# A new order of the steps in the start-up of a Mamba-2 and feed-forward kernel

## The reference

```python
x = x + _layernorm(mamba2(_layernorm(x)))        # in_proj, causal conv of 4 taps, SSM scan, gate, norm, out_proj
x = x + _layernorm(ffn(_layernorm(x)))           # 256 -> 2048 -> 256
```

## Time and profile before

| | us |
|---|---|
| three runs | 996.67, 999.93, 1002.15 |
| median | 999.93 |
| the profiled execution | 997.25 |
| its span | 995.5 |
| PE, DVE, ACT, POOL busy | 893.7, 776.1, 603.5, 341.3 |

### The profile page before, as it was taken

The page is one execution under the profiler, slowest core; times in us unless marked ns, Lnnn a source line. Parts: engine busy times, 40 slices in busy tenths (PEclk is TensorE's granted clock), DMA queues, the critical chain, the costliest instruction groups (busy, mean ns, idle before and its releaser), DMA issues.

```text
span 995.5 us, 17481 instructions
## 1 busy us (share of the span) xinstructions
PE 893.7 (90%) x6304; PEld 771.7 (78%) x6304; DVE 776.1 (78%) x2031; ACT 603.5 (61%) x1017; POOL 341.3 (34%) x342
## 2 busy tenths in 40 slices
...
DMA packets 19205, 34.57 MB, mean 35 GB/s; under 512 B 2480, under 2 KB 11440, under 8 KB 19120
## 3 DMA queue, kind: packets, MB, share of 16 engines
...
q10 hardware_dynamic: 864, 0.03, 0.1%
...
## 4 chain that ended last, share of the span: by engine, by line
PE 54%; DVE 22%; ACT 8%; issue 7%; POOL 5%; DMA 3%; SPq 0%; DVEq 0%; POOLq 0%; ACTq 0%
PE fb L1082 24%; PE db L1082 12%; PE mb L1082 10%; DVE xc L890 4%; DVE lmat L864 2%; PE mb L1191 2%; DMA lmat<-rows 2%; PE mb L1182 2%; DVE hid L999 2%; PE mb L1197 1%; POOL hl L588 1%; PE mb L1172 1%; POOL yg L576 1%; ACT hl L717 1%; DMA wg_raw<-in_packed 1%
## 5 line engine op out<-in xcount | busy, mean ns | idle before, releaser
L588 POOL TENSOR_TENSOR hl<-hid,hl 128x512 fp32r<-128x512 f32 (+1 forms) x144 | 171.2, 1189 | 415.3 <-ACT hl L717 415.3
L1082 PE MATMUL fb<-x1t,wg 128*128 128x512 f32 (+1 forms) x864 | 218.4, 389 | 5.2 <-DVE x1t L993 5.2
L1082 PE MATMUL db<-wd,hl 128*128 128x256 f32 x1536 | 213.7, 289 | 2.0 <-POOL hl L588 2.0
L1082 PE MATMUL fb<-x1t,wu 128*128 128x512 f32 (+1 forms) x864 | 205.0, 374 | 7.2 <-ACT hid L710 7.1
L1082 PEld LDWEIGHTS db<-wd,hl 128*128 128x128 f32 x1536 | 197.4, 191 | 16.7 <-issue 9.1
L1082 PEld LDWEIGHTS fb<-x1t,wu 128*128 128x128 f32 x864 | 151.6, 192 | 42.4 <-ACT hid L710 14.6
L1082 PEld LDWEIGHTS fb<-x1t,wg 128*128 128x128 f32 x864 | 148.1, 195 | 35.5 <-issue 8.7
L999 DVE TENSOR_TENSOR hid<-fb,hid 128x512 f32<-128x512 f32 (+1 forms) x144 | 90.4, 628 | 90.0 <-PE fb L1082 76.8
L717 ACT ACTIVATE hl<-hid 128x512 fp32r<-128x512 f32 (+1 forms) x144 | 83.6, 581 | 98.2 <-DVE hid L999 69.6
L890 DVE SCALAR_TENSOR_TENSOR xc<-raw,cw,xc 128x256 f32<-128x256 f32 x288 | 133.6, 532 | 8.2 <-ACT xc L663 7.0
L710 ACT ACTIVATE hid<-fb 128x512 f32<-128x512 f32 (+1 forms) x144 | 78.1, 548 | 78.2 <-PE fb L1082 75.0
(11 more groups left out here) (140 smaller groups left out, 1347.0 us busy)
## 6 DMA issues: line engine op xcount, KB each, us to landing
...
```

Source lines behind the costliest of these rows:

```text
L588: pool.tensor_tensor(hl[:, hs, n % 2, 1, :], hid[:, hs, n % 2, :], hl[:, hs, n % 2, 0, :].bitcast(F32), ALU.subtract).then_inc(s["lo"], 1)
L1082: last = pe.matmul(ps, lhs(a, k), rhs(b, k), start=start and n == 0, stop=stop and n == len(todo) - 1, skip_group_check=check)
```

## The change

The text of `FIRST` is written anew for PE, ACT, DVE and POOL. Each list holds the same steps as before, each of them once: 108 on PE, 145 on ACT, 154 on DVE, 46 on POOL. `ORDER`, `LAST` and all functions stay. The table is one line longer, so that every line behind it has a number one higher. One line of the diff, the first of ACT's list, as a sample:

```diff
@@ -102,47 +102,48 @@
 FIRST = {
...
     "act": """
-        wi_split:0 rates:0 dq:0 wi_z:0 xn_split:1 taps:3 dq:1 dq:2 gate:3 dq:3 dl:0 taps:4 dq:4 gate:4 dq:5 dq:6
...
+        wi_split:0 xn_split:1 wi_z:0 rates:0 taps:3 wo_split:0 dq:0 silu:3 taps:4 dq:1 gate:3 dt_bias:1 dq:2
...
```

More of the change, by code:

```diff
@@ L104 @@
     "pe": """
[L105 to L109, removed]
@@ L110 @@
-        yt:3> gu:14 dn:12 out:3> gu:15 x1t:0> dn:13 z:0>> z:1>> ip:0>> x1t:1> dn:14 ip:1>> dn:15 ip:2>> z:2>>""",
-    "act": """
-        wi_split:0 rates:0 dq:0 wi_z:0 xn_split:1 taps:3 dq:1 dq:2 gate:3 dq:3 dl:0 taps:4 dq:4 gate:4 dq:5 dq:6
[L113 to L125, removed]
@@ L126 @@
-    "dve": """
[L127 to L139, removed]
@@ new lines @@
+        xt:1 ip:3 ip:4 z:3 z:4 z:5 ip:5 cs:1 ct:1 xtr:2 gb:1 yo:2 st:2 yd:2 xt:0> xtr:3 yt:2 yo:3 out:2 yd:3
+        yt:3 st:3 out:3 z:0> z:1> ip:0> ip:1> ip:2> x1t:1 cs:0> z:2> gu:0 ct:0> gu:1 gu:2 xtr:0> yo:0> gb:0>
+        gu:3 yd:0> dn:0 st:0> dn:1 yt:0> xtr:1> gu:4 out:0> yo:1> dn:2 gu:5 yd:1> st:1> gu:6 xt:1> dn:3 yt:1>
+        dn:4 ip:3> gu:7 out:1> z:3> z:4> dn:5 gu:8 ip:4> ip:5> cs:1> dn:6 gu:9 z:5> ct:1> xtr:2> gb:1> gu:10
+        dn:7 xt:0>> dn:8 gu:11 yo:2> dn:9 st:2> yd:2> gu:12 xtr:3> yt:2> dn:10 gu:13 yo:3> out:2> dn:11 yd:3>
@@ new lines @@
+        gu:14 dn:12 yt:3> gu:15 st:3> out:3> z:0>> z:1>> x1t:0> dn:13 dn:14 ip:0>> ip:1>> z:2>> x1t:1> dn:15
+        ip:2>>""",
+    "act": """
+        wi_split:0 xn_split:1 wi_z:0 rates:0 taps:3 wo_split:0 dq:0 silu:3 taps:4 dq:1 gate:3 dt_bias:1 dq:2
+        gate:4 gate:5 dl:0 dq:3 dq:4 silu:4 dq:5 taps:5 dl:1 dq:6 dl:2 silu:5 dq:7 dq:8 dl:3 exps:1 decay_sums:4
+        decay_sums:5 decay_matrix:4 decay_matrix:5 gb_copy:1 decay_sums:6 decay_matrix:6 decay_sums:7
+        xn_split:0> square:2 yt_split:2 decay_matrix:7 square:3 yt_split:3 dq:9 dl:4 dt_bias:0> gate:0> taps:0>
+        gate:1> taps:1> x1_split:1 taps:2> gelu:0 gelu:1 split:0 dl:5 dl:6 gelu:2 gate:2> silu:0> silu:1>
+        silu:2> decay_sums:0> exps:0> decay_matrix:0> decay_sums:1> split:1 decay_matrix:1> decay_sums:2>
+        decay_matrix:2> gb_copy:0> decay_sums:3> decay_matrix:3> gelu:3 split:2 yt_split:0> square:0> dl:7 dq:10
+        split:3 dl:8 gelu:4 dl:9 gelu:5 split:4 gelu:6 xn_split:1> yt_split:1> split:5 taps:3> square:1> gelu:7
+        split:6 dl:10 dt_bias:1> split:7 gate:3> gate:4> gelu:8 taps:4> dq:11 taps:5> silu:3> gate:5> silu:4>
+        silu:5> gelu:9 split:8 decay_sums:4> gb_copy:1> decay_sums:5> gelu:10 decay_sums:6> exps:1> split:9
+        decay_matrix:4> decay_matrix:5> decay_sums:7> xn_split:0>> decay_matrix:6> split:10 decay_matrix:7>
+        gelu:11 square:2> split:11 gelu:12 yt_split:2> dl:11 gelu:13 split:12 gelu:14 yt_split:3> square:3>
+        split:13 gelu:15 split:14 dt_bias:0>> gate:0>> split:15 x1_split:0> gate:1>> taps:0>> x1_split:1>
+        taps:1>> taps:2>>""",
@@ new lines @@
+    "dve": """
+        stats1:1 xn:1 xn_split:1 wi_split:0 rates:0 wo_split:0 wo_lo:0 conv:3 dq:0 dt_bias:1 conv:4 stats1:0>
+        scale:0 dq:1 dq:2 scale:1 softplus:1 dq:3 scale:2 dq:4 decays:1 conv:5 dl:1 dl:2 xn:0> dq:5 dq:6 dq:7
+        scale:3 xdt:2 dl:3 scale:4 sums:1 dl:0 gb_copy:1 scale:5 yoff:2 decayed_products:2 dq:8 state:2 ydiag:2
+        xn_split:0> xdt:3 yt_split:2 decayed_products:3 yoff:3 stats2:2 ydiag:3 ln2:2 yt_split:3 state:3 dq:9
+        scale:6 stats2:3 x1n:2 dt_bias:0> ln2:3 softplus:0> x1n:3 conv:0> decays:0> x1_split:1 conv:1> inter:0
+        scale:7 inter:1 conv:2> sums:0> dl:5 dl:4 scale:8 xdt:0> gb_copy:0> yoff:0> inter:2 decayed_products:0>
+        stats1:1> scale:9 ydiag:0> state:0> decayed_products:1> yt_split:0> inter:3 xdt:1> xn:1> stats2:0> dq:10
+        yoff:1> inter:4 ln2:0> ydiag:1> state:1> xn_split:1> inter:5 scale:10 yt_split:1> inter:6 dl:6 x1n:0>
+        dl:7 stats2:1> inter:7 dt_bias:1> ln2:1> softplus:1> conv:3> decays:1> conv:4> conv:5> stats1:0>>
+        sums:1> inter:8 dq:11 gb_copy:1> inter:9 scale:11 xn:0>> dl:10 dl:8 dl:9 xdt:2> inter:10
+        decayed_products:2> yoff:2> xn_split:0>> state:2> ydiag:2> inter:11 xdt:3> yt_split:2> inter:12
+        decayed_products:3> yoff:3> inter:13 dl:11 stats2:2> ydiag:3> ln2:2> inter:14 yt_split:3> x1n:1>
+        state:3> inter:15 stats2:3> dt_bias:0>> x1n:2> ln2:3> x1_split:0> x1n:3> conv:0>> x1_split:1> fin:0
@@ L140 @@
         softplus:0>> ln4:0""",
     "pool": """
[L142 to L145, removed]
+        stats1:1 wi_split:0 stats1:0> xdt:2 yoff:2 xdt:3 yoff:3 stats2:2 ln2:2 stats2:3 ln2:3 split:0 xdt:0>
```

3 lines of the change are left out of this document (added).

## The result

The changed kernel takes **971.39 us** (median of 4 runs, 969.60 to 974.46), the kernel before 998.30 in the same session; the ratio is 0.973, interval [0.9687, 0.9772]. The forecast was 984.0 with a range from 973 to 993. So the direction was right, and the gain, 27 us, was too large for the range. It is on the side of rival 1, which had a chance of 0.12. The profiled execution took 970.84 us, its span is 969.1.

A forecast was written before the change was run, and what follows sets the result against it. PE bounds the loop, while the start up to `gu:0` of block 1 waits. A hand-counted 28.3 us lead less 12.6 lengthening gave 16 us; 997.25 less 16 is 981.25, plus 2.7 for the median: 984 us, range 973 to 993.

The forecast's parts named there:

- rival 1: Start, up to `gu:0` of block 1: DVE meets POOL less, gain 28.3 us, 971.6 by the median; chance 0.12.
- So I add the whole 12.6 back: Start: DVE's 12.6 us of lengthening kept in the new order, moving `gu:0` from 174.5 to 187.1.
- nothing met POOL: Upper bound of the start's gain: 28 us if DVE's instructions were not lengthened by POOL.
- DVE's idle time: Start: 26.4 left of 42.5 us idle, 16.1 less.
- `gu:0` near 187: First loop matmul of block 1 on PE starts near 187 us instead of 202.8.
- DVE's busy time unchanged near 164: Up to `gu:0`: DVE's busy time stays near 164 us; a fall to 155 would be the larger-gain case.
- The start: `ip:3` starts at 11.1 instead of 16.72, the first convolution at 17.8 instead of 24.94; 4.5 us gained.
- The first half of block 1: Four `decay_matrix` steps follow one table load; the lead is 24 us at `state:1`, 6 of them borrowed.
- The end: First convolution of block 2 fills DVE's 3.74 us wait for the last `x1_split`; `gu:0` at 174.5.
- rival 3: Feed-forward starves behind the scan if `inter:8` ends after about 148: slower, 1009 us; chance 0.05.
- Rival 2: Last 30 us of the start: PE partly at clock 0.5, 8 us less gain, 992 us; chance 0.13.
- The loop: From `gu:0` on: same instructions, entered 16 to 20 us earlier by each engine, counted as zero.

The follow-up runs named there:

- memset_before: Kernel before, POOL's `xdt` and `yoff` of blocks 0 and 1 and `split` of block 0 replaced by fills of about equal duration: 988.39 us, ratio 0.9901.
- thin_after: Changed kernel with most of POOL's wide work of blocks 0 and 1 left out (`xdt` after the first, `yoff`, part of `split`): 969.67 us, ratio 0.9694.
- memset pair: POOL steps of the first blocks replaced by write-only fills, in the old and the new order: 988.39 and 970.06 us.
- thin pair: POOL's wide steps of blocks 0 and 1 cut to a few columns, in the old and the new order: 982.89 and 969.67 us.
- new_to_26: Steps done by 26 us of the changed kernel in the new order, all others in the old order: 995.91 us, ratio 0.9976 to the kernel before.
- start_fix: Changed kernel with ACT's `wi_z` moved behind `rates` and `wo_split` ahead of `taps:3`: 970.29 us, ratio 0.9714 to the kernel before.
- mid_undone: Changed kernel with `gelu:3` and `split:2` back between ACT's second and third `decay_matrix`: 977.7 us, ratio 0.9784 to the kernel before.
- end_undone: Changed kernel with the last `x1_split` back ahead of the first convolution of block 2: 974.9 us, ratio 0.9755 to the kernel before.
- dodge: Kernel before with three DVE steps (`dq:10`, `scale:10`, `xn:0` of block 1) moved off their POOL neighbours: 994.21 us, ratio 0.995.

## Why the prediction was wrong

**The step that failed** is "So I add the whole 12.6 back", with the sentence ahead of it, that I see no reason why the new order should meet POOL less. It does: 4.5 us by the same measure. The measure leaves out one clash in the start of each order, 1.3 us before and 2.2 now. By the first number the forecast would have been 174.5 + 4.5 = 179.0 for `gu:0`, where the profiles have 177.87 and 175.70, and 24 us of gain, 976, inside the range. The rule that each microsecond of lengthening costs the path about one was right for the old order (memset_before: 9.7 less, `gu:0` 10.3 earlier); for the new one it isn't shown (thin_after: 3.2 us less busy, `gu:0` no earlier). The amount depends on which DVE step stands beside which POOL step, so it belongs to the order and not to the work, and 46 POOL steps would have had to be laid beside the new DVE list to count it. My bounds for the term named 28 for "nothing met POOL"; giving that end 0.12 and the middle 0.63 had no row behind it.

Counted out, the median came 12.6 us under the forecast of 984.0: 7.3 are DVE's busy time, 1.7 more idle time saved than the 16 forecast, 1.4 the part after `gu:0`, and 2.1 have nothing to do with the kernel (the median was put 2.7 above the profiled execution, and lay 0.55 above it). Without the failed step the rest would have landed inside the range. That 971.39 is so near rival 1's 971.6 is luck: `gu:0` came 25.0 us earlier and not 28.3, and clashes with POOL were still there; the last two terms made up the difference.

**Point by point.**
- DVE's idle time: forecast 16.1 us less, measured 17.7. Right, and borne out as a term of its own by the memset pair (18.3 us between the orders with POOL's reads gone), less so by the thin pair (13).
- `gu:0` near 187: wrong, 177.87.
- DVE's busy time unchanged near 164: wrong, 153.43 up to `gu:0`. The 164.5 had been read up to 207 us; up to `gu:0` it was 160.72, so the fall is 7.3 us and not 11. The text gave "falls to 155" as the sign of rival 1, and that is what came.
- The start: `ip:3` near 11 and convolution near 18: wrong by 2.3 and 2.4 us, the first from a single clash, the second behind it. It mattered little: the start alone gains 2.4 us (new_to_26), and start_fix isn't to be told from the changed kernel.
- The first half of block 1: `state:1` near 118, measured 119.15. Right, and mid_undone shows that the block of four `decay_matrix` matters, by 6.3 us; less by the loads than by the wait that stood between them.
- The end: the wait of 3.74 us for `x1t` fell to 0.6, but end_undone doesn't move `gu:0`; that part of the reasoning gave no gain at the place where it was counted, and whether it gave one behind it isn't shown.
- `inter:8`: by hand 136.4, measured 140.3, before 148: rival 3 didn't come. Rival 2 neither: PE's clock in the last stretch is 0.95, against 0.89 before.
- The loop: counted as zero, 1.4 us at most.

**Still open.** Why the new lists meet POOL less was not found step by step: `xn` alone accounts for 3.0 of the 12.6 us before and for none now, the rest is spread over the dequantization, `lmat`, the convolution and `mr`, and dodge shows that moving three steps gives little of it. Why the parts of the order give more together than alone is not explained in numbers. Of the 17.7 us of idle time only what mid_undone takes back, 6.3 us at `gu:0`, has an experiment of its own.
